# Y turned by VectorE squares and a trip through DRAM instead of TensorE transposes, from the second block on

## The reference

```
xn  = layernorm(x)
xz  = xn @ in_proj_w.T;  x_branch, z = split(xz)
s   = silu(causal_conv4(x_branch) + conv_b)
X, dt, B, C = split(s @ x_proj_w.T)
dt  = softplus(dt @ dt_proj_w.T + dt_proj_b)
Y   = ssd(X*dt, -exp(A_log)*dt, B, C) + X*D
attn = (Y * silu(z)) @ out_proj_w.T
hidden = sigmoid(xn @ q(w1).T) * (xn @ q(w2).T)       # q: ternary {-1, 0, 1}
out = x + attn + hidden @ q(w3).T
```

## Time and profile before

| | us |
|---|---|
| median of 3 runs (1664.38 to 1667.06) | 1666.37 |
| the profiled execution | 1663.81 |
| its span, first to last instruction | 1662.0 |
| PE busy | 1600.7 (96%) |
| DVE busy | 1126.5 (68%) |
| ACT busy | 895.1 (54%) |
| POOL busy | 540.0 (32%) |
| time of the hardware DMA queue's packets, of 16 engines | 16.5% |

### The profile page before, as it was taken

The page is one execution under the profiler, slowest core; times in us unless marked ns, Lnnn a source line. Parts: engine busy times, 40 slices in busy tenths (PEclk is TensorE's granted clock), DMA queues, the critical chain, the costliest instruction groups (busy, mean ns, idle before and its releaser), DMA issues.

```text
span 1662.0 us, 25592 instructions
## 1 busy us (share of the span) xinstructions
PE 1600.7 (96%) x9430; PEld 785.2 (47%) x9430; DVE 1126.5 (68%) x1812; ACT 895.1 (54%) x1848; POOL 540.0 (32%) x502
## 2 busy tenths in 40 slices
PE   7778899999999999999999999999999999999999
PEld 3333444544444444445444454445444444444544
DVE  7876786687566764687656885568755676467762
ACT  6775526465356644476354663647535565357541
POOL 5236673243033421244121441314303242133320
PEclk9889899999999999999999999999999999999999
DMA  7144340111002110112001110011100111002100
GB/s 259 53 145 158 121 146 13 53 64 51 1 26 59 45 52 1 40 58 58 26 7 46 56 48 26 7 59 55 46 15 26 59 45 52 1 27 71 58 1 26
DMA packets 49277, 89.72 MB, mean 54 GB/s; under 512 B 6112, under 2 KB 7904, under 8 KB 49152
## 3 DMA queue, kind: packets, MB, share of 16 engines
q1 hardware_dynamic: 49152, 88.08, 16.5%
HBM read 79.41 MB, written 8.65 MB: 53 GB/s over the span
## 4 chain that ended last, share of the span: by engine, by line
PE 77%; issue 6%; ACT 6%; DVE 5%; POOL 2%; DMA 1%; SPq 0%; DVEq 0%; ACTq 0%; POOLq 0%
PE bank L612 18%; PE bank L522 13%; PE bank L630 9%; PE bank L416 9%; PE bank L432 8%; PE bank L589 7%; PE bank L442 4%; ACT edc L851 3%; PE bank L554 2%; PE bank L566 2%; PE bank L579 1%; PE bank L539 1%; POOL less L1508 1%; DVE edc L1204 1%; DVE mdc L1210 1%
## 5 line engine op out<-in xcount | busy, mean ns | idle before, releaser
L522 PE MATMUL bank<-wx_hi,arena 128*128 128x512 f16 x1024 | 319.3, 382 | 0.0
L612 PE MATMUL bank<-xt_lo,q 128*128 128x512 f16 x704 | 266.8, 379 | 0.0
L612 PE MATMUL bank<-xt_hi,q 128*128 128x512 f16 x704 | 266.8, 379 | 0.0
L1476 POOL TENSOR_TENSOR xst<-xdt,dst 128x512 f32<-128x512 f32 x64 | 66.8, 1043 | 530.1 <-DVE xdt L1158 530.1
L522 PE MATMUL bank<-wx_lo,arena 128*128 128x512 f16 x512 | 195.7, 382 | 0.0
L630 PE MATMUL bank<-q,arena 128*128 128x512 fp8e4 x704 | 163.2, 380 | 0.0
L851 ACT ACTIVATE edc<-csl,csv 128x128 f32<-128x128 f32 x512 | 155.8, 389 | 0.6 <-DMA csl<-sums 0.6
L522 PEld LDWEIGHTS bank<-wx_hi,arena 128*128 128x128 f16 x1024 | 101.0, 99 | 114.6 <-issue 3.4
L884 ACT CAST arena<-full 128x512 f16<-128x512 f32 x88 | 54.6, 620 | 148.1 <-DVE full L1261 148.1
L1204 DVE TENSOR_TENSOR edc<-edc,gt 128x512 f32<-128x512 f32 x128 | 88.2, 729 | 63.6 <-ACT edc L856 63.5
L1261 DVE SCALAR_TENSOR_TENSOR full<-tnh,bank 128x512 f32<-128x512 f32 x88 | 60.4, 687 | 96.3 <-PE bank L612 95.7
(11 more groups left out here) (202 smaller groups left out, 3563.3 us busy)
## 6 DMA issues: line engine op xcount, KB each, us to landing
csl<-sums SPq DMA_DIRECT2D x128, 256.0 KB, 3.3
raw<-w_ffn SPq DMA_DIRECT2D x34, 256.0 KB, 3.0
res<-x SPq DMA_DIRECT2D x32, 256.0 KB, 4.0
out<-res SPq DMA_DIRECT2D x32, 256.0 KB, 2.0
full<-w_ffn SPq DMA_DIRECT2D x24, 256.0 KB, 3.9
yac<-x SPq DMA_DIRECT2D x16, 256.0 KB, 2.7
gate<-x SPq DMA_DIRECT2D x16, 256.0 KB, 3.2
arena<-w_in SPq DMA_DIRECT2D x4, 512.0 KB, 7.4
```

The lines of the kernel that those rows point to most:

```text
L522: i = pe.matmul(banks[0][:], act[:, k, c * P:(c + 1) * P], wt[:, k, hf * half:(hf + 1) * half], start=(n == 1), stop=(n == 3 * ki))
L612: i = pe.matmul(banks[2 * (m % 2) + j][:], q12[:, j, m, k, :], part[:, k, :], start=(n == 1), stop=(n == 2 * kd))
L1476: pool.tensor_tensor(by_head(xst[:], hd), by_head(xdt[:], hd), heads_over(sml["dst"][:, c, :], hf * hph, hph, hd), ALU.mult).then_inc(S["x ...
```

## The change

Block 0 stays as it was (its functions are now called `turn_first` and `project_first_out`). In blocks 1 to 7:

- PE makes no transposes of Y. DVE turns the gated Y of unit u in squares of 32x32 (`dve.transpose`, `yac[u % 2]` to `xs[u % 2]`), behind `project_x(u+1)` and ahead of `add_state(u)`. That puts the elements of each square in order, not the squares.
- SP moves the squares: in its unit u+1 it waits for DVE's transpose, writes `xs` to a buffer in DRAM (one per parity), waits until that has landed, and issues four reads, each of 32 partitions, in runs of 32 float32. They land in `yac[u % 2]`, for units 6 and 7 in `xs[u % 2]`. For unit 7 this stands after the loop over the units, ahead of the loads of the network.
- ACT and DVE split from that SBUF tile in place of PSUM bank 7. ACT's part of unit u-1 moves from the start of unit u to behind `update(u+1)`, DVE's to behind its `update(u+1)`; for unit 7 both go to step 4 of the network.
- The out projection goes by halves of 12 matmuls, two units behind: half u-2 at the end of unit u, the last two behind steps 2 and 6 of the network. DVE's residual add moves to the end of the odd units from 3 on, and to step 7.

```diff
+        ysq = [xs[u % 2] for u in range(len(units))]
+        yf = [yac[u % 2] if u < 6 else xs[u % 2] for u in range(len(units))]
+        y_dram = nc.dram_tensor("y_squares", [halves, P, half], F32, kind="Internal").ap()
+        def squares(dram, j):
+            return dram.rearrange("(i a) (k j b) -> j a k i b", a=SQ, b=SQ, j=P // SQ)[j]
+        def by_feature(t, j):
+            return t[j * SQ:(j + 1) * SQ, :].rearrange("a (k i b) -> a k i b", i=P // SQ, b=SQ)
...
 sync_program
+            def turn_y(b, u):
+                hf, n = u % 2, rounds(b, u)
+                sp.wait_ge(S["y_blocks"], at(b - 1, "y_blocks", u))
+                if n:
+                    sp.wait_ge(D[f"y_in{hf}"], n * (P // SQ) * DMA)
+                sp.dma_start(y_dram[hf], ysq[u][:]).then_inc(D[f"y_out{hf}"], DMA)
+                sp.wait_ge(D[f"y_out{hf}"], (n + 1) * DMA)
+                for j in range(P // SQ):
+                    sp.dma_start(by_feature(yf[u], j), squares(y_dram[hf], j)).then_inc(
+                        D[f"y_in{hf}"], DMA)
...
                     if u + 1 < len(units):
                         sums_in(b, u + 1)
+                    if b and u:
+                        turn_y(b, u - 1)
...
+                if b:
+                    turn_y(b, 7)
                 for m in range(kf):
...
 tensor_program
+            def project_out(b, u):
+                hf = u % 2
+                if u == 0:
+                    pe.wait_ge(S["acc"], at(b, "acc", 7))
+                elif hf == 0:
+                    pe.wait_ge(S["attn"], at(b, "attn", u // 2 - 1))
+                pe.wait_ge(S["yt_lo"], at(b, "yt_lo", u))
+                n = 0
+                for k in range(hf * per, (hf + 1) * per):
+                    for act, wt in passes(yt, wo):
+                        n += 1
+                        i = pe.matmul(banks[7][:], act[:, k, :], wt[:, k, :],
+                                      start=(hf == 0 and n == 1), stop=(hf == 1 and n == 3 * per))
                 i.then_inc(S["out_mm"], 1)
...
-                    if u and u % 2 == 0:
-                        project_out(b, u // 2 - 1)
+                    if b == 0 and u and u % 2 == 0:
+                        project_first_out(u // 2 - 1)
+                    elif b and u >= 2:
+                        project_out(b, u - 2)
...
+                    elif b and m in (2, 6):
+                        project_out(b, 6 if m == 2 else 7)
...
 scalar_program
+                    act.wait_ge(D[f"y_in{hf}"], (rounds(b, u) + 1) * (P // SQ) * DMA)
...
+                    src = yf[u][:]
+                act.mul(yt[0][:, hf * per:(hf + 1) * per, :], src.rearrange("p (k t) -> p k t", k=per),
+                        down).then_inc(S["yt_hi"], 1)
...
                         update(b, u + 1)
                     aside()
+                    if u and b:
+                        split_y(b, u - 1)
                     if u + 2 < len(units):
                         project_z(b, u + 2)
...
 vector_program
             def turn_y(b, u):
+                dve.wait_ge(S["y_gated"], at(b, "y_gated", u))
+                dve.transpose(ysq[u][:], yac[u % 2][:]).then_inc(S["y_blocks"], 1)
...
                         project_x(b, u + 1)
+                    if b:
+                        turn_y(b, u)
                     add_state(b, u)
                     if u + 1 < len(units):
                         update(b, u + 1)
                     aside()
-                    if u and u % 2 == 0:
+                    if b == 0 and u and u % 2 == 0:
                         project_out(b, u // 2 - 1)
+                    if u and b:
+                        split_y(b, u - 1)
                     if u + 2 < len(units):
                         project_z(b, u + 2)
                     split_state(b, u)
+                    if b and u >= 3 and u % 2:
+                        project_out(b, u // 2 - 1)
```

More of the change, by code:

```diff
@@ L121, in mamba_ffn_block @@
               *(f"early{n}" for n in range(4)),
-              *(f"beside{n}" for n in range(4)), "sums_out", "sums_in0", "sums_in1")}
+              *(f"beside{n}" for n in range(4)), "sums_out", "sums_in0", "sums_in1",
+             "y_out0", "y_out1", "y_in0", "y_in1")}
         def sb(name, shape, dt=F32):
@@ L257, in load_x @@
                     if c < 2:
-                        sp.wait_ge(S["y_turned"], at(b - 1, "y_turned", 6 + c))
+                        if b == 1:
+                            sp.wait_ge(S["y_turned"], 7 + c)
+                        else:
+                            sp.wait_ge(S["y_blocks"], at(b - 2, "y_blocks", 6 + c))
                     else:
@@ L682, in tensor_program @@
                     aside()
-                    if u:
-                        turn_y(b, u - 1)
+                    if u and b == 0:
+                        turn_first(u - 1)
                     aside()
@@ L702, in tensor_program @@
                     ffn_up(b, m)
[L703 to L706, removed]
+                    if b == 0 and m == 0:
+                        turn_first(7)
+                    elif b == 0 and m == 1:
+                        project_first_out(3)
+                    elif b and m in (2, 6):
+                        project_out(b, 6 if m == 2 else 7)
                 if b < nb - 1:
@@ L811, in project_x @@
                 act.wait_ge(S["x_mm"], at(b, "x_mm", u))
-                if u >= 2:
+                if u >= 2 and b:
+                    act.wait_ge(D[f"y_out{u % 2}"], rounds(b, u) * DMA)
+                elif u >= 2:
                     act.wait_ge(S["y_skip"], at(b, "y_skip", u - 2))
@@ L863, in decay, with split_y @@
                     act.mul(mdc[2 * (u % 2) + g][:, 0, :], edc[g][:], M_SCALE / B_SCALE ** 2).then_inc(S["m_hi"], 1)
[L865 to L873, removed]
-                hf = u % 2
-                act.mul(yt[0][:, hf * per:(hf + 1) * per, :],
-                        banks[7][:].rearrange("p (k t) -> p k t", k=per), down).then_inc(S["yt_hi"], 1)
+            def split_y(b, u):
+                hf = u % 2
+                if b == 0:
+                    act.wait_ge(S["y_turned"], u + 1)
+                    if hf == 0 and u:
+                        act.wait_ge(S["first_out"], u // 2)
+                    src = banks[7][:]
+                else:
+                    act.wait_ge(D[f"y_in{hf}"], (rounds(b, u) + 1) * (P // SQ) * DMA)
+                    if u >= 2:
+                        act.wait_ge(S["out_mm"], at(b - 1, "out_mm", u - 2))
+                    elif b == 1:
+                        act.wait_ge(S["first_out"], chunks)
+                    else:
+                        act.wait_ge(S["out_mm"], at(b - 2, "out_mm", 6 + u))
+                    src = yf[u][:]
+                act.mul(yt[0][:, hf * per:(hf + 1) * per, :], src.rearrange("p (k t) -> p k t", k=per),
+                        down).then_inc(S["yt_hi"], 1)
             def hid_hi(b, m):
@@ L996, in scalar_program @@
                         aside()
-                    if m == 0:
-                        turn_y(b, 7)
+                    if m == (4 if b else 0):
+                        split_y(b, 7)
                 if b < nb - 1:
@@ L1218, in before_chunk @@
                     dve.wait_ge(S["dst"], at(b, "dst", 0))
-                if u >= 2:
-                    dve.wait_ge(S["y_turned"], at(b, "y_turned", u - 2))
+                if u >= 2 and b == 0:
+                    dve.wait_ge(S["y_turned"], u - 1)
+                elif u >= 2:
+                    dve.wait_ge(S["yt_lo"], at(b, "yt_lo", u - 2))
                 else:
@@ L1240, in turn_y @@
                 dve.wait_ge(S["yt_hi"], at(b, "yt_hi", u))
+                src = yf[u][:] if b else banks[7][:]
                 dve.scalar_tensor_tensor(
-                    out=yt[1][:, ks, :], in0=banks[7][:].rearrange("p (k t) -> p k t", k=per),
+                    out=yt[1][:, ks, :], in0=src.rearrange("p (k t) -> p k t", k=per),
                     scalar=down, in1=yt[0][:, ks, :], op0=ALU.mult,
@@ L1409, in vector_program @@
                         aside()
-                    if m == 0:
-                        turn_y(b, 7)
-                    if m == 1:
+                    if m == (4 if b else 0):
+                        split_y(b, 7)
+                    if m == (7 if b else 1):
                         project_out(b, 3)
```

33 lines of the change are left out of this document (21 added, 12 removed).

## The result

The changed kernel takes 1692.23 us (median of 4 runs, 1690.9 to 1695.12) against 1665.38 for the kernel before beside it (1664.14 to 1667.06): a ratio of 1.0166, 95% interval 1.0154 to 1.0179. It is slower by 27 us; the forecast was 9.7 us faster. The profiled execution took 1695.12, with a span of 1693.0.

The account below looks back on a forecast made before the run. PE's issued work plus its few waits was taken to bound each block; the steps summed to 1.39 us per block, 9.7 over seven, taking the median from 1666.37 to 1656.7 us (forecast range 1654 to 1662, overall 1644 to 1670).

Parts of the forecast that it names:

- The transpose: DVE's new operation between xdt_lo and state: 0.69 us assumed, 0.61 to the next start, with ends 0.49 and 0.89.
- Step 1: scan(1) of a block stays where it is, since PE's transposes only filled its wait: gain 0.
- Step 2: scan(2) waits for the other engines' loop of 11.1 us, 0.12 later than before; PE's wait about 1.3.
- Step 3: Units 3 to 6: PE last at 12.36 us, loop 11.1 or 11.7; 2.18 gained, plus 0.5 in unit 7.
- Step 4: scan(7): unit 6 has no z product, so PE waits 0.24 us for the operands.
- Step 5: update(7): xst_lo ends 2.06 us after xdt_lo, PE has only 0.70 to do: a new wait of 1.36.
- Step 6: Network: one set of transposes less, 0.44 us; the two projection halves cost what the whole did.
- DVE's idle time: DVE's 56 transposes (34 us) otherwise lie in the 32% of the time that DVE is idle.
- Round trip: DRAM write and four reads, from transpose's end to last read: L = 8.6 us, with room to 10.0, costing nothing.
- rival A: The DRAM trip outlasts its cover, first at ACT's wait for y_in(6): slower, 1676 to 1756 us; chance 0.17.
- the ceiling: The loop doesn't hold scan(2) and update(7), or the projection's spread helps more: 20 to 24 us, 1642 to 1646; chance 0.11.
- Rival B: No difference: a transpose of 1.2 us, or another wait of about a microsecond per block: 1665 us; chance 0.14.

Follow-up runs that it names:

- experiment 1: Changed kernel without SP's trip through DRAM, ACT and DVE splitting the unturned Y: 1692.63 us, 1.0169 of the kernel before.
- experiment 3: Changed kernel with DVE's gate of the next unit and residual add behind yoff, ahead of the mask multiplies: 1657.09 us, 0.9957 of the kernel before.
- experiment 4: Changed kernel with POOL's skip add on only 16 of 512 columns in blocks 1 to 7: 1654.48 us, 0.9941 of the kernel before.
- experiment 7: Changed kernel with gate and residual add behind yoff and the transpose between xst_lo and yt_lo: 1653.0 us, 0.9936 of the kernel before.
- experiment 8: Changed kernel with POOL's state scaling on 2 of each head's 64 columns in blocks 1 to 7: 1652.74 us, 0.993 of the kernel before.
- experiment 2: Changed kernel with DVE's transpose covering only 32 of 512 columns: 1667.59 us, 1.0019 of the kernel before.

## Why the prediction was wrong

- **The transpose** (taken as 0.69, 0.61 to the next start): right, 0.70 and 0.63.
- **Step 1**, no gain at scan(1): right.
- **Step 2**, the loop in short units, 11.1: wrong, 11.74 from xdt_lo(1) to xdt_lo(2), and 12.12 and 12.72 in the units behind, where step 3 took 11.1 and 11.7. **This is the term that failed**, "11.0+0.61-0.49 = 11.1": it carried all other durations over from before, though 0.97 for xdt_lo "beside a busy POOL" stood in the same section. Moving yt_hi did bring ACT's exponential forward, and the idle 0.53 ahead of the multiplies went. But DVE, rid of yt_lo there, then met the skip add: +0.80 on the pair, +0.39 on xst_lo, +0.18 on the low parts of the decay behind the pair, with 0.25 of state_lo given back.
- **Step 3**, "PE is last": PE's 12.36 was right, and PE has no gap in units 3 to 6. But the loop of 12.12 and 12.72 is level with it on average (12.42) instead of 1 us below, so DVE comes to unit 7 with hardly any lead.
- **Step 4**, scan(7) 0.24: 2.44. Unit 6's own PE work is 9.77, and the loop of 12.71 no longer fits in it.
- **Step 5**, update(7) 1.36: 1.64, the rest being xst_lo's wait for POOL.
- **Step 6**, the network: no transposes there, as said. But the clock behind the two waits was left out: 3.26 - 1.73 = 1.53 in this block.
- **DVE's idle time**, "its 32%": that is a mean over stages. From scan(2) to scan(7) DVE was busy 51.39 of 64.51 us before (80%) and is 57.66 of 61.79 now (93%); most of its idle time lies in the network, where no transpose could use it.
- **Round trip**: right that it is hidden, by experiment 1. L was 6.4, under the 8.6 taken. ACT did sit microseconds on y_in(6), 5.16, which the prediction named as a sign of rival A, and it cost nothing. The first statistics behind it wait 1.31 for the x loads ("about 1 us"), which PE doesn't feel.

By starts, the sum closes. A wait is counted here from where the next matmul would have started, 0.17 more than the idle time of the rows: 1.98 at scan(2), 2.61 at scan(7), 1.79 at update(7). Against the forecast block of 196.93, scan(2) loses 0.64 more, scan(7) 2.37, update(7) 0.43, the clock 1.53: 4.97, and 201.90 against a measured 201.83. Experiments 3, 4, 7 and 8 show the collisions as the cause; the clock's share is set apart by the one block of experiment 2, at about 1.5.

The three rivals named the round trip, a dearer transpose, and the ceiling; none asked what else would run beside the moved operations. Rival B came closest in form (a transpose of 1.2 us, "For: xdt_lo at 0.97 beside POOL") but put the loss on the transpose, which has one input and is at 0.70 wherever it stands.

The Trainium skill (SBUF — State Buffer, Who interferes with whom) states the rule that should have been a rival: a VectorE instruction with two SBUF inputs contends with a GpSimd instruction that reads SBUF, one with at most one does not. It calls what they contend for an exclusive lock, so that the later one waits for the whole of the other. The trace agrees on both. Gate and yoff take 0.68 and the transpose 0.70 in the loops, beside POOL or not. The operations with two SBUF inputs take about 0.68 with POOL idle; where one comes behind an operation of POOL it ends 0.55 us after POOL's, whether it is recorded as 0.97 (xdt_lo), 1.32 (xst_lo) or 1.76 long (the second multiply), in every such case of blocks 2 to 7 of both kernels. A long record is therefore a wait, and its length is read from where the other engine's operation ends.

## What to carry to other kernels

When a DVE operation is moved or inserted, write POOL's timeline beside DVE's and ask anew which operations with both inputs in SBUF now meet it, and which comes first; their durations don't move with them. xst_lo took 0.93 while it began 0.34 ahead of POOL's scaling, and 1.32 when it began 0.27 behind. An operation that reads PSUM (0.68 here), or has one input (the transpose, 0.70), is the right filler for the place beside a POOL operation, and the right order can be worth more (39 us here) than the work removed. Where two engines' loops are within a few per cent of one another, a microsecond on the shorter one is no longer hidden, and its waits can lower TensorE's clock on top.

## What the runs showed of the hardware

- A pair of 128x512 f32 multiplies in SBUF takes 1.29 behind the short add of experiment 4, and 2.36 where a 128x512 add of POOL gets in between the two: the add waits for the first (1.65 in place of 1.28), the second for the add.
- After waits of 2.44 and 1.64 us with 0.7 of work between them, TensorE was granted 0.50 for 3.3 us of unbroken work; behind the single wait of 1.82 at scan(2) the matmuls start 0.22 apart, at a granted clock of 1.00. Equal waits do not always have the same outcome: those of 1.65 and 0.64 in experiment 2 were followed by a lowered clock in one of six blocks.
- 126,336 more packets took 0.242 x 16 x 1693 - 0.165 x 16 x 1662 = 2168 us of the queue; less the 7168 of 2 KB at 0.089, that leaves some 13 ns for each run of 128 bytes (an estimate), where I had taken 30. A read of 32 partitions in such runs costs SP 0.65 us to issue (2.60 for four) against 0.45 for the x load in the earlier trace rows.
- A 32x32-square transpose of 128x512 f32 takes DVE 0.70, one of 128x32 0.20.
